# Smoothing in a graph kernel: two of ten blocks scaled by VectorE, loads two rows ahead, spilled edges two tiles at once

## What is computed

```python
src, dst, w = _gcn_norm(edge_index, edge_weight, n)
gamma = 1.0 / (2.0 * (1.0 - LAMBDA_AMP))
hh = x
for _ in range(K):
    lx = x - _spmm(x, src, dst, w, n)
    y = x - gamma * 2.0 * (1.0 - LAMBDA_AMP) * lx
    x = hh + _proximal_l21(y - hh, gamma * LAMBDA_AMP)
return x
```

## Time and profile before

| | |
|---|---|
| median of three runs | 8615.32 us |
| the profiled execution's own time | 8620.85 us |
| its span, first to last instruction | 8619.2 us |
| smoothing, first look-up to last step | 4546.6 to 6413.3 us |
| busy over the whole span | PE 81%, weight loads 68%, VectorE 69%, ScalarE 53%, POOL 33% |
| loaded per chunk | 2 x 320 KB |
| table, cleared rows, read-back, per pass | 1562.5, 1593.8 and 1562.5 KB |

### The profile page before, as it was taken

The page is one execution under the profiler, slowest core; times in us unless marked ns, Lnnn a source line. Parts: engine busy times, 40 slices in busy tenths (PEclk is TensorE's granted clock), DMA queues, the critical chain, the costliest instruction groups (busy, mean ns, idle before and its releaser), DMA issues. The chain is left out here.

```text
span 8619.2 us, 280713 instructions
## 1 busy us (share of the span) xinstructions
PE 6966.2 (81%) x98149; PEld 5903.7 (68%) x98174; DVE 5906.5 (69%) x15840; ACT 4550.4 (53%) x14713; POOL 2850.0 (33%) x2937
## 2 busy tenths in 40 slices
PE   0299999999999899999956886877867787875876
PEld 0155555555555699999956776877867777875866
DVE  1277676766777699898966886886885555555555
ACT  0222222222222499999956997987974444433443
POOL 0078888888888655454530000000000000000000
PEclk9999999999999999999978998999988898987978
DMA  9222222222222377777747887887965454542534
GB/s 385 89 57 61 59 59 60 58 61 58 60 59 59 110 233 232 225 231 223 232 141 232 285 281 244 286 280 253 290 208 167 164 171 157 179 156 90 182 126 134
DMA packets 781195, 1429.84 MB, mean 166 GB/s; under 512 B 294298, under 2 KB 361580, under 8 KB 776696
## 3 DMA queue, kind: packets, MB, share of 16 engines
q1 hardware_dynamic: 571720, 967.63, 36.0%
q10 hardware_dynamic: 116928, 381.29, 12.8%
q0 software_dynamic: 92048, 74.42, 4.4%
HBM read 987.87 MB, written 433.30 MB: 165 GB/s over the span
## 5 line engine op out<-in xcount | busy, mean ns | idle before, releaser
L243 POOL DMA_INDIRECT sorted_rows<-sort_rows,sort_row_at x1600 | 1989.5, 1243 | 518.4 <-issue 507.1
L1458 ACT ACTIVATE smooth_msg<-smooth_ps_l,smooth_w_rows 128x64 f32<-128x64 f32 x7500 | 1592.1, 404 | 229.0 <-PE smooth_ps_l L1522 215.4
L272 ACT ACTIVATE sort_count<-sort_ps_c 50x50 bf16<-50x50 f32 x1600 | 331.2, 207 | 1995.4 <-PE sort_ps_c L304 1559.0
L1216 PE MATMUL poly_ps<-parts,poly_cast 125*128 125x192 bf16 x12500 | 1088.5, 252 | 201.9 <-DVEq L1295 106.3
L1216 PEld LDWEIGHTS poly_ps<-parts,poly_cast 125*128 125x128 bf16 x12500 | 1071.6, 100 | 218.6 <-issue 135.4
L1182 ACT ACTIVATE poly_cast<-poly_mat 128x1280 bf16<-128x1280 uint8 x500 | 609.3, 1262 | 767.9 <-PE poly_ps L1216 520.0
L1522 PE MATMUL smooth_ps_l<-parts,smooth_src 125*128 125x64 bf16 x22500 | 798.5, 194 | 260.5 <-DMA smooth_src<-src_rows 163.7
L1522 PEld LDWEIGHTS smooth_ps_l<-parts,smooth_src 125*128 125x128 bf16 x22500 | 717.7, 99 | 298.0 <-ACT smooth_msg L1458 110.9
L314 PE MATMUL sort_ps_m<-sort_w,sort_hidden 128*125 128x64 f32 x3200 | 879.3, 430 | 0.0
L1536 PE MATMUL smooth_ps_s<-smooth_msg,smooth_hot 128*128 128x64 bf16 x7500 | 760.3, 194 | 143.7 <-DVE smooth_last_part L1670 119.0
L300 PEld LDWEIGHTS sort_ps_r<-sort_count,sort_hot_dt 50*125 50x125 bf16 x1600 | 283.0, 177 | 847.2 <-issue 643.8
(11 more groups left out here) (312 smaller groups left out, 14702.1 us busy)
## 6 DMA issues: line engine op xcount, KB each, us to landing
smooth_src<-src_rows SPq DMA_DIRECT2D x750, 320.0 KB, 4.3
smooth_hot<-hot_rows SPq DMA_DIRECT2D x750, 320.0 KB, 4.7
poly_mat<-counts_t ACTq DMA_DIRECT2D x504, 400.0 KB, 3.6
sorted_rows<-zeros ACTq DMA_DIRECT2D x100, 875.0 KB, 13.2
graph_edges<-sorted_rows SPq DMA_DIRECT2D x125, 700.0 KB
conv_mat<-counts ACTq DMA_DIRECT2D x208, 400.0 KB, 3.6
hot_rows<-graph_hot SPq DMA_DIRECT2D x125, 640.0 KB, 3.4
src_rows<-graph_hot_t SPq DMA_DIRECT2D x125, 640.0 KB, 3.7
```

The lines of the kernel that those rows point to most:

```text
L243: pool.indirect_dma_start(out=sorted_rows, out_offset=bass.IndirectOffsetOnAxis(row_at[u][:, j:j + 1], 0), in_=rows[u][:, j, :], in_offset ...
L1216: last = nc.tensor.matmul(ps[u][:, 0:3 * D], cast[u][h][0:NL, s, :], parts[:, b].rearrange("p i d -> p (i d)"), start=b == 0, stop=b == NB ...
L1458: last = act.activation(at[:, s, :], ps_l[g % 2][h][:, i * D:(i + 1) * D], ACT.Copy, scale=w_rows[:, u, c * CHUNK + s:c * CHUNK + s + 1])
```

## The change

ScalarE scales eight of a chunk's ten blocks, from a PSUM bank of their own (`ps_a`); VectorE scales the other two (`ps_v`) with one product of 128 x 128, `scale`, issued for the next chunk right behind a chunk's first subtraction, over the boundaries of rows and pairs too. `add_up` lies three chunks behind the look-up. The matrices have buffers for two rows, filled with four transfers a row (`LOADS`: two of 20 slots, two of 30) that wait for the row before the last. Weights are copied a row at a time. The edges from a node to itself become three matmuls per row against the identity (`ident16`), and `post` has 14 steps instead of 15 (9 instead of 10 in the last pass). The post-processing loop now covers pairs 4 to 21, and pairs 22, 23 and 24 have two rounds each. The spilled edges' code moves into a class `Spilled`, which takes two tiles per round (`n_pairs` rounds, here one); the table is written from ScalarE's queue after row 0 of a pass; the result rows are cleared at the stage's start and then right behind each read-back. The sort pads one more tile of rows and computes `n_pairs`. `hh` becomes a view of `node_sums` (64 of each 66 columns), and the second set of parts shares memory with sums and rest.

```diff
-                pool.indirect_dma_start(
-                    out=sorted_rows, out_offset=bass.IndirectOffsetOnAxis(pad_at[:, 0:1], 0),
-                    in_=zeros[0:TE, 0:ROW], in_offset=None,
-                    bounds_check=N_SLOTS + SPILL_ROWS - 1, oob_is_err=False).then_inc(padded, 16)
+                for i in two:
+                    pool.indirect_dma_start(
+                        out=sorted_rows, out_offset=bass.IndirectOffsetOnAxis(pad_at[:, i:i + 1], 0),
+                        in_=zeros[0:TE, 0:ROW], in_offset=None,
+                        bounds_check=N_SLOTS + SPILL_ROWS - 1, oob_is_err=False).then_inc(padded, 16)
...
+BY_ACT = 8
+
+LOADS = ((0, 20), (20, 50))
...
+    def write_table(self, eng, xs):
+
+        eng.dma_start(self.rows.rearrange("(p b) d -> p (b d)", b=NB), xs[:].rearrange("p b d -> p (b d)"))\
+           .then_inc(self.table, 16)
...
+    def clear(self, pool, first):
+        if first:
+            pool.memset(self.zeros[:], 0.0).then_inc(self.cleared, 1)
+            pool.wait_ge(self.cleared, 1)
+        pool.dma_start(self.y_rows.rearrange("(p z b) c -> p z (b c)", z=self.ZB, b=YB // self.ZB),
+                       self.zeros[:].unsqueeze(1).to_broadcast([TE, self.ZB, YB // self.ZB * D])).then_inc(self.zeroed, 16)
...
+    def on_pool(self, pool, k, n, y_sb):
+        pool.wait_ge(self.table, 16 * k + 16)
+        pool.wait_ge(self.zeroed, 16 * k + 16)
+        with pool.Fori(0, n) as t:
+            m = k * n + t
+            pool.dma_start(self.edges[:], self.sorted_rows[bass.ds(N_SLOTS + t * (2 * TE), 2 * TE), :]
+                           .rearrange("(i p) c -> p i c", i=2)).then_inc(self.got, 16)
+            pool.wait_ge(self.got, m * 16 + 16)
+            pool.sem_inc(self.taken, 1)
+            pool.tensor_copy(self.from_at[:], self.edges[:, :, self.gather]).then_inc(self.ids, 1)
+            pool.wait_ge(self.ids, m + 1)
+            pool.sem_inc(self.taken, 1)
+            for i in range(2):
+                pool.indirect_dma_start(out=self.of_node[:, i, :], out_offset=None, in_=self.rows,
+                                        in_offset=bass.IndirectOffsetOnAxis(self.from_at[:, i:i + 1], 0))\
+                    .then_inc(self.fetched, 16)
+            pool.wait_ge(self.ready, m + 1)
+            pool.sem_inc(self.taken, 1)
+            for i in range(2):
+                pool.indirect_dma_start(out=self.y_rows, out_offset=bass.IndirectOffsetOnAxis(self.to[:, i:i + 1], 0),
+                                        in_=self.total[:, i, :], in_offset=None, compute_op=ALU.add)\
+                    .then_inc(self.added, 16)
+                pool.wait_ge(self.added, m * 32 + (16 * i + 16))
+                pool.sem_inc(self.taken, 1)
+        pool.dma_start(y_sb[:].rearrange("p b d -> p (b d)"),
+                       self.y_rows[0:N_NODES, :].rearrange("(p b) c -> p (b c)", b=NB)).then_inc(self.y_in, 16)
...
-    ADD = 2
-
-    SPILL_AT, LATE, TWICE = 1, 3, 23
+    ADD = 3
+
+    SPILL_AT, LATE, TWICE = 1, 4, 22
...
-        hot = [sb(f"hot{c}", [128, HALF, 128, 2], BF16) for c in range(N_CHUNKS)]
-        src = [sb(f"src{c}", [128, CHUNK, 128], HOT) for c in range(N_CHUNKS)]
-        w_rows = sb("w_rows", [128, 2, NB], F32)
+        hot = [[sb(f"hot{u}{i}", [128, (b - a) // 2, 128, 2], BF16) for i, (a, b) in enumerate(LOADS)] for u in two]
+        src = [[sb(f"src{u}{i}", [128, b - a, 128], HOT) for i, (a, b) in enumerate(LOADS)] for u in two]
+        w_rows = [sb(f"w_rows{u}", [128, NB], F32) for u in two]
...
+                def load(row, u, i):
+                    a, b = LOADS[i]
+                    sp.dma_start(src[u][i][:].rearrange("p s d -> p (s d)"),
+                                 src_rows[row, :, a:b, :].rearrange("a p s d -> (a p) (s d)")).then_inc(src_in[u][i], 16)
+                    sp.dma_start(hot[u][i][:].rearrange("p s d v -> p (s d v)"),
+                                 hot_rows[row, :, a:b, :].rearrange("a p s d -> (a p) (s d)")).then_inc(hot_in[u][i], 16)
+
+                def rows_from(p, k):
+
+                    for u in two:
+                        for i in two:
+                            sp.wait_ge(chunk_done, 2 * N_CHUNKS * p + (N_CHUNKS * (k * NB + u - 2) + LOADS[i][1] // CHUNK))
+                            sp.sem_inc(taken, 1)
+                            load(bass.ds(2 * p + u, 1), u, i)
...
+                    spilled.on_pool(pool, k, n, y_sb)
+                    pool.wait_ge(spilled.y_in, 16 * k + 16)
+                    if k < PASSES - 1:
+                        spilled.clear(pool, False)
...
-                    for h in two:
-                        act.wait_ge(looked, 2 * number + (h + 1))
-                        for i in range(HALF):
-                            s = h * HALF + i
-                            last = act.activation(at[:, s, :], ps_l[g % 2][h][:, i * D:(i + 1) * D], ACT.Copy,
-                                                  scale=w_rows[:, u, c * CHUNK + s:c * CHUNK + s + 1])
-                        last.then_inc(scaled, 1)
+                    act.wait_ge(looked_a, number + 1)
+                    for i in range(BY_ACT):
+                        last = act.activation(at[:, i, :], ps_a[g % 2][:, i * D:(i + 1) * D], ACT.Copy,
+                                              scale=w_rows[u][:, c * CHUNK + i:c * CHUNK + i + 1])
+                    last.then_inc(scaled_a, 1)
...
+                        if isinstance(p, int) and p == 0 and u == 0:
+                            act.wait_ge(posted, PAIRS * (k + 1))
+                            spilled.write_table(act, xs)
...
+                    for ps, first, end, scaled, looked in ((ps_a, 0, BY_ACT, scaled_a, looked_a),
+                                                           (ps_v, BY_ACT, CHUNK, scaled_v, looked_v)):
                         if not (isinstance(number, int) and number < 2):
-                            pe.wait_ge(scaled, 2 * number + (h - 3))
-                        for i in range(HALF):
-                            b = h * HALF + i
+                            pe.wait_ge(scaled, number - 1)
+                        for i in range(first, end):
+                            t, at = part_of(c * CHUNK + i)
                             for j in range(3):
-                                last = nc.tensor.matmul(ps_l[g % 2][h][:, i * D:(i + 1) * D], src[c][0:NL, b, :],
-                                                        parts[k % 2][:, c * CHUNK + b, j, :], start=j == 0,
-                                                        stop=j == 2, skip_group_check=True)
+                                last = nc.tensor.matmul(ps[g % 2][:, (i - first) * D:(i - first + 1) * D],
+                                                        src[u][t][0:NL, at, :], parts[k % 2][:, c * CHUNK + i, j, :],
+                                                        start=j == 0, stop=j == 2, skip_group_check=True)
...
+                    if c == 0:
+
+                        for j in range(3):
+                            own = parts[k % 2][:, row - k * NB, j, :] if isinstance(row, int) else \
+                                parts[k % 2][:, bass.ds(u + 2 * p, 1), j, :].rearrange("p a d -> p (a d)")
+                            nc.tensor.matmul(ps_s[u][:, 0:D], ident16[0:NL, :], own, start=j == 0, stop=False)
...
-                    link(dve.tensor_tensor(z[:], z[:], xs[:, b, :], ALU.add))
...
+                def scale(k, p, u, c):
+                    number = N_CHUNKS * row_of(k, p, u) + c
+                    dve.wait_ge(looked_v, number + 1)
+                    if c == 0:
+                        dve.wait_ge(w_kept, row_of(k, p, u) + 1)
+                    if not (isinstance(number, int) and number < RING):
+                        dve.wait_ge(chunk_done, number - (RING - 1))
+                    dve.tensor_tensor(msg[c][:, BY_ACT:CHUNK, :],
+                                      ps_v[(u * N_CHUNKS + c) % 2][:, 0:(CHUNK - BY_ACT) * D].rearrange("p (s d) -> p s d", d=D),
+                                      w_rows[u][:, c * CHUNK + BY_ACT:(c + 1) * CHUNK].unsqueeze(2)
+                                      .to_broadcast([128, CHUNK - BY_ACT, D]), ALU.mult).then_inc(scaled_v, 1)
...
-                            dve.wait_ge(scaled, 2 * number + 2)
+                            dve.wait_ge(scaled_a, number + 1)
+                            dve.wait_ge(scaled_v, number + 1)
                             dve.tensor_tensor(rest[c][:], msg[c][:], high(msg[c]), ALU.subtract).then_inc(firsts, 1)
+                            if c + 1 < N_CHUNKS or u == 0:
+                                scale(k, p, u + (c + 1) // N_CHUNKS, (c + 1) % N_CHUNKS)
+                            elif not isinstance(p, int) or p < PAIRS - 1:
+                                if not (isinstance(p, int) and p == SPILL_AT):
+                                    scale(k, p + 1, 0, 0)
+                            elif k < PASSES - 1:
+                                scale(k + 1, 0, 0, 0)
```

(3 more changed lines are left out.)

273 lines of the change are left out of this document (143 added, 130 removed).

## The result

The changed kernel takes **8466.85 us** (median of 4 runs, 8463.98 to 8469.93) against 8612.14 for the kernel before on the same chip (4 runs): a ratio of 0.9832, 95% interval [0.9815, 0.9849]. That is 145 us, where 95 were forecast. The profiled execution took 8463.98 us with a span of 8462.3.

The account below looks back on a forecast made before the run. ScalarE was taken as nearest to full, VectorE and loads close behind, with stalls in pairs 0 to 3. Terms 6.8 - 19.4 + 16.6 - 100.6 + 1.5 = -95.1 took 8620.85 to 8525.8, less 5.5 = 8520 us; range 8465 to 8605.

Parts of the forecast that it names:

- rival 4: Loads do better in larger pieces, 340 GB/s: pairs 0 to 3 -27, pass 2 -8, table writes -20; 8465 us; chance 0.12.
- The gap behind a step: VectorE's post-processing, loop pairs: each step priced 0.43 us, gap included; 23.1 us a pair, +6.8 in passes 0 and 1.
- The wait of 0.66 us at a pair's start: VectorE in loop pairs: read as waiting for ScalarE; 0.55 taken off, leaving 21.4 us of own work a pair.
- Second and third semaphore, +0.25: VectorE, each chunk's first subtraction in pairs 4 to 21: extra semaphores cost 0.25 us a pair, between 0 and 0.9.
- Product at 0.20 to its successor: VectorE's ten new products a pair: each 0.29 us long, 0.21 in the queue; two dependent gaps filled, -0.2 a pair.
- Loads in pass 2: Pairs 4 to 21 of pass 2: loads limit at 307 GB/s, 21.3 us a pair; 21.5 taken, -19.4 us.
- Lead and sums: Longer load lead, worth PE's 22.9 us of waits, counted within other cases; sums 3 chunks behind: 0.
- Pairs 0 to 3: Start of each pass: loads rule, spilled edges stay once; 101, 107, 107 us, 315 against 415.6, -100.6.
- rival 1: VectorE's products do not overlap: 1.0 us more a pair, +55 us, 8575; chance 0.14.
- rival 2: Table write, read-back and clearing contend as before: pairs 0 to 3 +8 a pass, clearing +10 each; 8564; chance 0.12.
- rival 3: Slower: VectorE's products wait for PE's look-ups; 55 us per 0.1 us a chunk, 8670 at 0.25; chance 0.07.
- rival 5: Spilled edges: POOL comes late, PE and VectorE wait beside idle work; up to 10 us a pass, 8550; chance 0.03.

Follow-up runs that it names:

- run 2: Changed kernel with semaphore thresholds counted in threes and twos, so a register instruction stands between a step's wait and the next subtraction: 8559.51 us, 0.9944.
- run 3: Kernel before, with one semaphore for each half of ScalarE's scaling, so the step's wait need not sit on a register instruction: 8582.96 us, 0.997.
- run 12: Changed kernel with 320 KB loads, VectorE scaling only in some chunks, and an already met look-up wait elsewhere: 8412.36 us, against 8437.31 without that wait.
- run 1: Changed kernel, but ScalarE scales all ten blocks of each chunk and VectorE has no product: 8464.56 us, 0.9836.
- run 7: Changed kernel with rows loaded in five pieces of 320 KB, still two rows ahead: 8451.39 us, 0.9817.
- run 9: Changed kernel with the result rows cleared at the start of the next pass instead of behind the read-back: 8488.19 us, 0.986.
- run 5: Changed kernel with five 320 KB loads a row, one row of lead instead of two, and sums 2 chunks behind: 8593.54 us, 0.9985.
- run 8: Changed kernel with self edges added on VectorE again as one more step, without the six matmuls a pair on PE: 8487.04 us, 0.9857.

## Why the prediction was right, and where it was not

The sign, the range (at its edge: 8467 against 8465) and the engine that becomes the bound in passes 0 and 1 were right. The sum was 50 us short, nearly all in one stretch. That the range held was luck: its lower end is rival 4's 8465, which was added up from faster pairs 0 to 3 (another -27, where they came out 12 slower than forecast) and covered table writes, while the time came from the loop.

- **The gap behind a step was the term that failed.** The 23.1 us a pair took the step of 0.43, gap included, from the trace of before as a property of the step. The gap belonged to the register instruction behind it: the two thresholds (2n+2 and n+1) had to be computed in turn, and the step's wait stood on that computation. The change made all thresholds n+1 or n+2. At 0.09 and 0.10 us for the fourteen steps this is 1.3 us a pair. In passes 0 and 1, 36 pairs by 1.2 us (23.1 forecast, 21.9 measured) are 43, of which the long pair 4 takes some 15 back. In pass 2, where only nine steps stand, it is 0.9 us a pair, and the ceiling of the loads had hidden VectorE altogether (below). The same trace had the answer: the forecast itself took 0.35 a step for pairs 22 to 24 from the earlier trace rows, where there is no loop, and that term came out right. The instruction streams that stand ahead of the prediction showed it (`REGISTER_ALU [waits step]` before, `[waits firsts,step]` on the subtraction after), and I did not price it. Runs 2, 3 and 12 show it: +93, -24 and -25 us for edits that change no work.
- **The wait of 0.66 us at a pair's start was misread.** The prediction took 0.55 of it off VectorE's own work as a wait for ScalarE, as the view names it. But ScalarE's last block for the subtraction at 5699.43 had ended at 5698.88 by the trace's records, and the gap is 0.65 to 0.66 in every loop pair of passes 0 and 1, whenever ScalarE ended. It is the end of the loop again, 0.62 after the change. So "VectorE's own work" was 21.95 and not 21.4. This error and the next two hide part of the first: 23.1 - 1.3 + 0.55 - 0.25 - 0.1 = 22.0, against 21.9.
- **Second and third semaphore, +0.25**: nothing in the loop, where the waits are taken while the subtraction before still runs: in a chunk without a step the next first subtraction starts 0.73 behind the second one's start, against 0.74 before.
- **Product at 0.20 to its successor**: right in the queue, but in a chunk without a step it costs 0.07: 1.67 us a chunk here against 1.60 before, where the second subtraction waited for the first (0.86 from start to start). The prediction had that as two gaps filled; there are three a pair. And with a step behind it, it pays part of its price by having the next threshold ready. Its removal gave only 0.5 us a pair in run 1, since the threshold was then late again and ScalarE is full there, 382 us busy of 389. The Trainium skill, which the prediction cites on this (VectorE: DVE Perf Modes, The DRAIN you can't avoid), says in the same paragraph that a next instruction that is not held starts earlier. The prediction left that out; the starts at 0.74 and 0.20 are such earlier ones.
- **Loads in pass 2**: the ceiling of 307 GB/s, 21.3 us a pair, was wrong. 6.55 MB in 19.7 us are 333 GB/s, at a share of 0.89; it had given 290 at 0.90. In pair 5 of pass 2 (5845.8 to 5865.0 us), behind the long pair 4, it is 363 at 0.97. And VectorE, not the loads, bounds pass 2: with steps 0.10 cheaper, my 21.05 would have been 20.1. Rival 4 foretold the time of 8465 and about this rate, by other parts of the sum; its reason, larger transfers, fell in run 7. The Trainium skill (DMA: Bandwidth & Descriptors, Bandwidth) advises 1 MiB and more for a transfer; here 320 KB pieces ran at the same 330 GB/s, at a share of 0.95 instead of 0.89, and the kernel was 15 us faster with them.
- **Lead and sums**: "worth PE's 22.9 us of waits, which I count in the cases above and not again" and "sums 3 chunks behind: 0" supposed a VectorE that never waits. But the lead and the sums are what makes it so: undone together they cost 127 us, the sums alone 49. The 0 was thus no price: a term of nothing that others stand on should have been told as such.
- **Pairs 0 to 3**: -88 against -100.6: 107.5, 107.6 and 110.3 us instead of 101, 107 and 107. The gap at the spilled edges is 6.4 against the 5.2 forecast. Pair 3 takes 28 to 30 us and pair 4 26 to 30 in all passes, in pass 2 too, where nothing is cleared; and run 9, without the clearing there, still has them at 28 to 29 and 24 to 29. So the clearing costs them some 7 us in all, and what else holds them stays open. The kernel is 21 us better with it there than at the start (run 9). Of the 88 us, undoing the lead and the sums takes back 49 (run 5 has 374 us in these pairs against 413 before); the other 40 belong to what that run keeps, the clearing's place, the table's write and the two tiles at once among it; no run undoes the last two alone. TensorE's granted clock was 0.86 to 0.90 on average in these pairs (0.84 and 0.85 before), against 1.00 in the loop; what that costs no run separates either.
- **Pairs 22 to 24**: +13 against +16.6; 26.3 a pair against 26.6, which is 13.15 a half against the 13.3 forecast from the earlier trace rows.
- **Self edges**: 0.43 a pair forecast, 0.24 to 0.34 measured in the loop (run 8): a step of 0.28 with its gap of 0.03 now.
- **Rivals**: 1 fell (0.20, never 0.28); 2 came in part (pairs 0 to 3 12 us over the forecast, the clearing behind the read-back 7); 3 fell (0.7 us of waits in sixteen pairs); 5 fell (one round, ScalarE idle for 6.4 us, and POOL, with both tiles gathered, waits 16 to 20 us for VectorE's totals).
- **"Nearly all of it comes from the stalls of pairs 0 to 3, not from the scaling"**: half right. Not from the scaling: run 1. But 68 of 145 us came from the loop, by steps that became cheaper and loads and sums that were no longer late, and each of these shows only with the others: the direct steps are worth 24 us in the kernel before and 93 here by run 2, whose gaps ahead of the first subtraction are wider than those of before; at the gaps of before I estimate 62 (1.3 us in 36 pairs, 0.9 in 18).

What stays open: what makes pairs 3 and 4 long; what taking two tiles at once and the later write of the table are worth by themselves; and why small pieces gain 15 us.

## What to carry to other kernels

On an engine that runs short instructions, look at what carries the wait between them. A threshold that can be computed before the producer ends must not be computed after it; use one threshold for all semaphores of a step, or compute it early by a wait that is already met. When a view names an engine as the end of a wait, check when that engine was done: a gap of the same length in every round is rather the waiting engine's own. And when one engine becomes the bound, undo each part alone and all covers together: here the part that stands first in the change's name was worth nothing, and without two that stood in the sum without a price of their own, the lead and the distance of the sums, 127 of its 145 us are gone.

## What the runs showed of the hardware that I had not expected

- A wait for a small step's semaphore costs 0.03 to 0.04 us on VectorE where it sits on the next tensor instruction itself, 0.12 to 0.15 where it sits on a register instruction ahead of it, and 0.19 to 0.23 where two such instructions stand between (in run 2 the second is a wait for two more semaphores; behind the reduction of L1727 they are the signal to ScalarE and a wait).
- The end of a loop costs VectorE 0.60 to 0.83 us a round in these kernels where the round's last instruction is a step that must be waited for, and nothing where it isn't (pass 2 of the changed kernel, where the loop's instructions are done while the subtraction before still runs).
- Loads ran at 330 GB/s with pieces of 320 KB (share 0.95) and of 640 and 960 KB (share 0.89), where the kernel before had 290 at 0.90. One pair ran at 363 (share 0.97). The share tells little of what rate is left, and between these sizes the size didn't set the rate.
- The sort stage, in which POOL's 1600 scatters take 1234 to 1243 ns each, ends up to 18 us apart between the profiled executions of these kernels, also between kernels with the same sort. A profile's own time should be held against the median before its stretches are compared.
